# Linear attention of a transformer block: rolled tile loop and zero-padded value windows, or rounds over tiles with nine-column value matmuls

## The reference, cut to what matters

```python
x = x + _L0_attn_ref(_layernorm(x, axis=-1), L0_attn_Wqkv, L0_attn_bqkv, L0_attn_Wout, L0_attn_bout, L0_attn_proj)

def _L0_attn_ref(x, Wqkv, bqkv, Wout, bout, proj):     # H = 16 heads of D = 8, M = 64 features
    ...
    q_prime = jax.nn.relu(jnp.einsum('bhtd,hdm->bhtm', qf, pf))
    k_prime = jax.nn.relu(jnp.einsum('bhtd,hdm->bhtm', kf, pf))
    k_cumsum = jnp.cumsum(k_prime, axis=2)
    kv_prod = jnp.einsum('bhtm,bhtd->bhtmd', k_prime, vf)
    kv_cumsum = jnp.cumsum(kv_prod, axis=2)
    context = jnp.einsum('bhtm,bhtmd->bhtd', q_prime, kv_cumsum)
    norm = jnp.einsum('bhtm,bhtm->bht', q_prime, k_cumsum)
    out = context / (norm[..., None] + 1e-06)
    ...
    return out @ Wout.T + bout
```

## Time and profile before

| | us |
|---|---|
| median of 3 runs | 5663.83 |
| lowest and highest | 5661.9, 5679.79 |
| profiled execution, its own time | 5654.4 |
| its span in the trace | 5652.5 |
| the stage, from line 263 at 1096.98 to the end of line 2151 at 1733.37 | 636.4 |
| one round, 31 steps of line 2151 from 1138.1 to 1733.1 | 19.2 |

### The profile page before, as it was taken

One profiled execution on the slowest core, in us unless ns is written; L12 is line 12 of the kernel. 1 busy time (PEld: TensorE's weight loads), 2 busy tenths in 40 slices (PEclk: granted clock), 3 DMA queues, 4 the chain that ended last, 5 costly groups with the idle time before them and its releaser, 6 DMA issues.

```text
span 5652.5 us, 141251 instructions
## 1 busy us (share of the span) xinstructions
PE 4905.5 (87%) x49788; PEld 3894.9 (69%) x49788; DVE 3263.9 (58%) x9577; ACT 2087.9 (37%) x5175; POOL 1829.5 (32%) x2766
## 2 busy tenths in 40 slices
PE   5999999877878999999593999876999998986999
PEld 4777777677775777767462777665667777874776
DVE  4777777634344666656442666586456656765333
ACT  1444444311111444422130555442245554542333
POOL 2555555300000333323404334494023434430000
PEclk8999999999998999989695999897989998886999
DMA  5000000000000100000022111000310100004665
GB/s 189 18 18 18 19 18 18 10 0 0 0 0 12 31 29 29 25 1 0 23 69 54 31 33 34 16 0 2 89 35 30 34 27 0 0 0 78 143 145 134
DMA packets 112405, 199.22 MB, mean 35 GB/s; under 512 B 13315, under 2 KB 54660, under 8 KB 111260
## 3 DMA queue, kind: packets, MB, share of 16 engines
q1 hardware_dynamic: 108147, 188.67, 12.8%
q0 software_dynamic: 4096, 8.40, 0.5%
HBM read 183.29 MB, written 18.97 MB: 36 GB/s over the span
## 4 chain that ended last, share of the span: by engine, by line
PE 65%; issue 17%; DVE 7%; ACT 4%; POOL 3%; SPq 1%; DMA 1%; POOLq 1%; another core or an unknown queue 0%; DVEq 0%; ACTq 0%
PE psum_banks L2996 6%; PE psum_banks L555 6%; PE psum_banks L3005 6%; PE psum_banks L560 5%; PE psum_banks L620 4%; PE psum_banks L664 3%; PE psum_banks L671 3%; PE psum_banks L1623 3%; PE psum_banks L624 3%; PE psum_banks L1658 2%; PE psum_banks L1084 2%; PE psum_banks L2677 2%; PE psum_banks L1599 2%; ACT scratch L1741 1%; PE psum_banks L1072 1%
## 5 line engine op out<-in xcount | busy, mean ns | idle before, releaser
L787 DVE TENSOR_REDUCE scratch<-psum_banks 128x2 f32<-128x514 f32 x768 | 531.4, 692 | 406.9 <-PE psum_banks L555 402.9
L560 PE MATMUL psum_banks<-scratch 32*128 32x128 f32 x6144 | 637.6, 309 | 8.1 <-ACT scratch L706 6.1
L706 ACT ACTIVATE scratch<-psum_banks 128x512 f32<-128x512 f32 x768 | 458.7, 597 | 488.1 <-PE psum_banks L565 477.1
L555 PE MATMUL psum_banks<-scratch 32*128 32x257 f32 x3072 | 574.0, 440 | 50.8 <-DVE scratch L788 50.8
L560 PEld LDWEIGHTS psum_banks<-scratch 32*128 32x128 f32 x6144 | 475.0, 185 | 17.3 <-ACT scratch L706 8.6
L3005 PEld LDWEIGHTS psum_banks<-w_L_ffn_down,scratch 128*128 128x128 f32 (+1 forms) x2560 | 336.7, 193 | 165.1 <-issue 141.2
L555 PEld LDWEIGHTS psum_banks<-scratch 32*128 32x128 f32 x3072 | 253.9, 188 | 272.2 <-issue 172.7
L2996 PE MATMUL psum_banks<-scratch,w_L_ffn_up 128*128 128x512 f32 (+1 forms) x752 | 382.7, 604 | 8.3 <-DVE scratch L3167 6.0
L3052 ACT ACTIVATE scratch<-psum_banks 128x512 f32<-128x512 f32 x344 | 205.4, 597 | 485.0 <-PE psum_banks L2996 485.0
L3167 DVE TENSOR_TENSOR scratch<-scratch 128x512 f32<-128x512 f32 x304 | 210.3, 692 | 294.7 <-ACT scratch L3052 272.6
L565 PE MATMUL psum_banks<-shift_T,own_batch 32*128 32x128 bf16 x3072 | 350.5, 214 | 0.0
(11 more groups left out here) (475 smaller groups left out, 12748.6 us busy)
## 6 DMA issues: line engine op xcount, KB each, us to landing
scratch<-route_T SPq DMA_DIRECT2D x136, 512.0 KB, 7.1
scratch<-in_ctx SPq DMA_DIRECT2D x99, 514.0 KB, 3.5
scratch<-in_ctx_rows SPq DMA_DIRECT2D x130, 128.0 KB, 2.0
scratch<-route_T SPq DMA_DIRECT2D x8, 1024.0 KB, 8.3
expert_rows<-in_ctx SPq DMA_DIRECT2D x10, 512.0 KB, 17.5
scratch<-expert_rows SPq DMA_DIRECT2D x16, 192.0 KB, 2.7
expert_out<-scratch SPq DMA_DIRECT2D x16, 192.0 KB, 2.1
w_L_ffn_up<-in_L_ffn_up SPq DMA_DIRECT2D x1, 2992.0 KB
```

Of the source, the lines that this page charges most:

```text
L555: return pe.matmul(S[:, g % 2, :], qbd[q, t.odd, (s // 2) * P:(s // 2 + 1) * P], kT_of[q, t.odd, s // 2, :], start=True, stop=True)
L560: return pe.matmul(W[:, g % 2, c * P:(c + 1) * P], kT_of[q, t.odd, b, c * P:(c + 1) * P], qbd[q, t.odd, b * P:(b + 1) * P], start=True, st ...
L706: act.activation(pT[:, b % 2, 2 * h:2 * h + 2].rearrange("p t c q -> p t (c q)"), W, ACT.Exp).then_inc(exp_ready.sem, 1)
L787: dve.tensor_reduce(parts[:, r.t.odd, 2 * h:2 * h + 2, 0, b], S, X_AXIS, ALU.max, negate=True)
```

## The change

`linear_attention` is written anew; nothing else in the program changes.

- Values: each head's masked products `am` (128 x 128) are now the weights at rest, and nine columns stream past: the head's 8 value columns and a column of ones, from `v0` or `v1` (written by turns; the ones are set once). One group of 16 matmuls (`weigh`) gives numerators and denominators, tokens on the partitions, 16 x 9 columns in bank 6. `vz`, the window of ones, and the second group of 16 are gone.
- Since tokens are now on the partitions, the heads are transposed by TensorE (`turn_heads`) and copied by ScalarE (`take_heads`) ahead of the output matmul, which gives tokens on the partitions as before.
- VectorE divides with a 128 x 16 reciprocal instead of 128 x 128, and adds the output straight to `x`; the bias is added to `x` by GpSimd earlier (`biased`). ScalarE, not VectorE, takes the transposed norm out of PSUM (`take_x`).
- Products and masks go in halves: `multiply(t, 0)` and `multiply(t, 1)` fill one bank for the even and one for the odd heads each, and the mask is four instructions of 512 columns. `weigh` runs in four groups of four heads, each after its own mask, and the q features in two halves, each after the masks that have read its bank.
- The loop is unrolled into rounds -2 to 32: in round r TensorE works on x of tile r+2, features and v of tile r+1, products and values of tile r, transposed heads and output of tile r-1. All four uses of bank 7 have quarters of their own, yet `bank_free` still lets only one writing or reading of the bank be open at a time, in the order x, heads, v, out.

```diff
...
-def linear_attention(k, s):
...
+def linear_attention(k):
...
+    HEADS = O[:, 0:H * W].rearrange("p (h c) -> p h c", c=W)
+    values = (a["v0"], a["v1"])
+    X_AT, HEADS_AT, V_AT, OUT_AT = (slice(P * n, P * n + P) for n in range(4))
+
+    cols = lambda n: slice(n * P, (n + 1) * P)
+    there = lambda t: 0 <= t < TILES
+
+    def bank_of(odd, s):
+        return k.bank[(0 if odd else 4) + s]
+
+    events, order = {}, 0
+    for r in range(-2, TILES + 1):
+        for name, t in (("x", r + 2), ("heads", r - 1), ("v", r + 1), ("out", r - 1)):
+            if there(t):
+                order += 1
+                events[name, t] = order
...
+            if t:
+                pool.wait_ge(xn.sem, xn.at(t))
+                pool.tensor_tensor(k.X[:, t - 1, :], k.X[:, t - 1, :], bo[:, :], ALU.add).then_inc(biased.sem, 1)
...
-        with pe.Fori(0, TILES) as i:
-
-            pe.wait_ge(sg["q_features_ready"].sem, sg["q_features_ready"].at(i, 0))
-            pe.wait_ge(sg["k_features_ready"].sem, sg["k_features_ready"].at(i, 0))
-            for c in range(chunks):
-                for odd in range(2):
-                    rows = slice(64 * odd, 64 * odd + 64)
-                    mm = pe.matmul(product_bank(2 * c + odd), s["feature"][rows, 1, cols(c)], s["feature"][rows, 0, cols(c)],
-                                   start=True, stop=True, skip_group_check=True)
-                    if c == chunks - 1:
-                        mm.then_inc(sg["products_written"].sem, 1)
-            next_x(i)
-            features(1)
-            pe.wait_ge(sg["masked"].sem, sg["masked"].at(i, 2))
-            features(0)
-            pe.wait_ge(misc.r.sem, misc.r.at(i, 0))
-            for n in range(2):
-                for h in range(heads):
-                    if n == 0:
-                        left = s["vz"][:, 120 * h + 120:120 * h + 120 + P]
-                    else:
-                        left = k.c("head_window")[:, 120 - 8 * h:120 - 8 * h + P]
-                    mm = pe.matmul(O[:, cols(n)], left, s["am"][:, 8 * (h % 2) + h // 2, :],
-                                   start=(h == 0), stop=(h == heads - 1), skip_group_check=True)
-            mm.then_inc(sg["pv_done"].sem, 1)
-            next_v()
-            pe.wait_ge(sg["heads_ready"].sem, sg["heads_ready"].at(i, 1))
-            pe.wait_ge(misc.r.sem, misc.r.at(i, 2))
-            pe.matmul(M[:, 0:P], s["outT"][:, 0, :], wo[:, :], start=True, stop=True).then_inc(misc.w.sem, 1)
...
+        def bank_free(name, t):
+            if events[name, t] > 1:
+                pe.wait_ge(read.sem, read.at(events[name, t] - 1))
...
+        def turn_heads(t):
+            pe.wait_ge(heads_ready.sem, heads_ready.at(t + 1))
+            bank_free("heads", t)
+            pe.transpose(M[:, HEADS_AT], a["heads"], k.c("ident")).then_inc(written.sem, 1)
+
+        def project_v(t):
+            bank_free("v", t)
+            pe.wait_ge(read.sem, read.at(events["x", t]))
+            pe.matmul(M[:, V_AT], a["xT"][:, t % 2, :], wv[:, :], start=True, stop=True).then_inc(written.sem, 1)
+
+        def out(t):
+            bank_free("out", t)
+            pe.wait_ge(read.sem, read.at(events["heads", t]))
+            pe.matmul(M[:, OUT_AT], a["headsT"], wo[:, :], start=True, stop=True).then_inc(written.sem, 1)
...
+        def k_features(t):
+            pe.wait_ge(read.sem, read.at(events["x", t]))
+            if t:
+                pe.wait_ge(k_ready.sem, k_ready.at(t))
+            for c in range(F):
+                mm = pe.matmul(k.bank[2 + c // 4][:, cols(c % 4)], a["feature_w"][:, 1, cols(c)], a["xT"][:, t % 2, :],
                                start=True, stop=True, skip_group_check=True)
-            mm.then_inc(sg["q_features_written" if n == 0 else "k_features_written"].sem, 1)
-
-        pe.wait_ge(sg["proj_ready"].sem, sg["proj_ready"].before(1))
+            mm.then_inc(k_written.sem, 1)
+
+        def q_features(t, s):
+            if t:
+                pe.wait_ge(masked.sem, masked.at(4 * (t - 1) + 2 * s + 2))
+            for c in range(4 * s, 4 * s + 4):
+                mm = pe.matmul(k.bank[s][:, cols(c % 4)], a["feature_w"][:, 0, cols(c)], a["xT"][:, t % 2, :],
+                               start=True, stop=True, skip_group_check=True)
+            mm.then_inc(q_written.sem, 1)
+
+        def multiply(t, s):
+            if s == 0:
+                pe.wait_ge(k_ready.sem, k_ready.at(t + 1))
+            pe.wait_ge(q_ready.sem, q_ready.at(2 * t + s + 1))
+            for c in range(4 * s, 4 * s + 4):
+                for odd in range(2):
+                    rows = slice(64 * odd, 64 * odd + 64)
+                    mm = pe.matmul(bank_of(odd, s)[:, cols(c % 4)], a["feature"][rows, 1, cols(c)], a["feature"][rows, 0, cols(c)],
+                                   start=True, stop=True, skip_group_check=True)
+            mm.then_inc(products.sem, 1)
+
+        def weigh(t, n):
+            odd, s = parts[n]
+            pe.wait_ge(masked.sem, masked.at(4 * t + n + 1))
+            if n == 0:
+                pe.wait_ge(read.sem, read.at(events["v", t]))
+                if t:
+                    pe.wait_ge(heads_ready.sem, heads_ready.at(t))
+            for j in range(4):
+                h = 2 * (4 * s + j) + odd
+                mm = pe.matmul(HEADS[:, h, :], a["am"][:, 8 * odd + 4 * s + j, :], values[t % 2][:, h, :],
+                               start=True, stop=True, skip_group_check=True)
+            if n == 3:
+                mm.then_inc(heads_done.sem, 1)
...
+        for r in range(-2, TILES + 1):
+            if there(r):
+                multiply(r, 0)
+            if there(r + 2):
+                turn_x(r + 2)
+            if there(r):
+                multiply(r, 1)
+            if there(r + 1):
+                k_features(r + 1)
+            if there(r - 1):
+                turn_heads(r - 1)
+            if there(r):
+                weigh(r, 0)
+                weigh(r, 1)
+            if there(r + 1):
+                project_v(r + 1)
+                q_features(r + 1, 0)
+            if there(r):
+                weigh(r, 2)
+            if there(r - 1):
+                out(r - 1)
+            if there(r):
+                weigh(r, 3)
+            if there(r + 1):
+                q_features(r + 1, 1)
...
+        def take_heads(t):
+            act.wait_ge(written.sem, written.at(events["heads", t]))
+            act.activation(a["headsT"], M[:, HEADS_AT], ACT.Copy).then_inc(read.sem, 1)
...
+        for r in range(-2, TILES + 1):
+            if there(r + 2):
+                take_x(r + 2)
+            if there(r - 1):
+                take_heads(r - 1)
+            if there(r + 1):
+                q_features(r + 1, 0)
+                q_features(r + 1, 1)
...
-        with dve.Fori(0, TILES) as i:
-            chain.round(i)
-            norm.dve_stats(dve, chain, i)
-            norm.dve_apply(dve, i)
-            for odd in range(2):
-                dve.wait_ge(sg["products_written"].sem, sg["products_written"].at(i, odd + 1))
-                b = 4 if odd == 0 else 0
-                dve.tensor_tensor(s["am"][:, 8 * odd:8 * odd + 8, :].rearrange("p (a n) q -> p a n q", a=2),
-                                  k.psum[:, b:b + 2, :].rearrange("p a (n q) -> p a n q", q=P),
-                                  bc(bc(k.c("causal_T"), 1, 4), 1, 2), ALU.mult).then_inc(sg["masked"].sem, 1)
-                if odd == 0:
-                    prep_x(i)
-            k_features(i)
-            dve.wait_ge(sg["pv_done"].sem, sg["pv_done"].at(i, 1))
-            prep_v(i)
-            link(dve.tensor_scalar(s["den"][:, :], O[:, P:2 * P], 1e-6, None, ALU.add))
-            link(dve.reciprocal(s["den"][:, :], s["den"][:, :]))
-            dve.tensor_tensor(s["outT"][:, 0, :], O[:, 0:P], s["den"][:, :], ALU.mult).then_inc(sg["heads_ready"].sem, 1)
-            dve.wait_ge(misc.w.sem, misc.w.at(i, 3))
-            dve.tensor_tensor(s["tmp"][:, :], M[:, 0:P], bo[:, :], ALU.add).then_inc(misc.r.sem, 1)
-            dve.wait_ge(misc.r.sem, misc.r.at(i, 3))
-            x = k.X[:, i, :]
-            link(dve.tensor_tensor(x, x, s["tmp"][:, :], ALU.add))
...
+        def mask(t, n):
+            odd, s = parts[n]
+            if odd == 0:
+                dve.wait_ge(products.sem, products.at(2 * t + s + 1))
+            dve.tensor_tensor(a["am"][:, 8 * odd + 4 * s:8 * odd + 4 * s + 4, :], bank_of(odd, s).rearrange("p (n q) -> p n q", q=P),
+                              bc(k.c("causal_T"), 1, 4), ALU.mult).then_inc(masked.sem, 1)
...
+        def divide(t):
+            dve.wait_ge(heads_done.sem, heads_done.at(t + 1))
+            link(dve.tensor_scalar(a["den"], HEADS[:, :, 8], 1e-6, None, ALU.add))
+            link(dve.reciprocal(a["den"], a["den"]))
+            dve.tensor_tensor(a["heads"].rearrange("p (h d) -> p h d", h=H), HEADS[:, :, 0:8], bc(a["den"], 2, 8), ALU.mult
+                              ).then_inc(heads_ready.sem, 1)
+
```

(51 more changed lines are left out.)

131 lines of the change are left out of this document (67 added, 64 removed).

## The result

| | before | after |
|---|---|---|
| median of 4 runs, us | 5662.86 | 5401.63 |
| lowest and highest | 5656.76, 5679.79 | 5398.66, 5424.59 |
| span of the profiled execution | 5652.5 | 5396.9 |
| the stage in the trace | 636.4 | 384.4 |

The ratio is 0.9543, with a 95% interval of 0.951 to 0.9576. The forecast was 5405 within 5348 to 5461. Of the 255.6 us that the span lost, 252.0 are in the stage; the other 3.6 lie in parts that nobody touched.

A forecast was written before the change was run, and what follows sets the result against it. The prediction took TensorE's own work plus its waiting gaps to bound the stage. Set-up 22.2, 31 round steps x 11.2 = 347 and last tile 8.5 gave 378 us against 636.4, hence 5405 us, range 5348 to 5461.

The forecast's parts named there:

- set-up to the first products: Start of the stage until TensorE's first products: 22.2 us, against 23.4 before, as the head projection now leads.
- 31 round steps: Steady rounds of the unrolled loop: 10.5 us at full clock, 11.2 at clock 0.94, 347 us in all.
- last tile: End of the stage, no features behind it: products, masks, values about 5.5, then divide to residual 3; 8.5 us.
- The matmuls: TensorE per round: products 1.86, features, v and output 4.03, transposes 0.22, 32 nine-column instructions at 0.108, 3.46 us.
- rival A: Nine-column matmuls on TensorE are cheap, 0.058 instead of 0.108 us each: round 9.5, stage 325, total 5352 us; 8%.
- Hand-overs and the stall: TensorE per round: 13 semaphore waits at 0.055, 0.72 us, plus 0.2 waiting for ScalarE's late q features.
- The gaps: TensorE's old waits ahead of transpose 1.00, features 0.93 and output 1.97, together 3.9 us a round; nearly none remain.
- rival B: Bank 7 becomes the chain, TensorE waiting for its readers, a 1.97 us gap: round 13.3, stage 443, total 5470; 11%.
- The clock: TensorE's mean clock in the new rounds: 0.94, between two other stages' 0.85 and 1.00, making 10.5 us 11.2.
- my bound: Slow end of the main case: hand-overs 0.1 each and clock 0.85, round 13.0, stage 434, total 5461 us.
- C: Nine-column groups drop TensorE's clock to 0.50 for the whole stage: round 21 us, stage about 685, total 5712; 2%.
- D: Unrolled code arrives late or rounds do not overlap: round 17 us or more, total 5580 to 5680; 3%.

The follow-up runs named there:

- the last experiment: Against the changed kernel: 32 columns per head, both q feature groups moved right behind v, both product groups together with the norm's transpose behind them; 5338.93 us, ratio 0.9466.

## Why the prediction was right

The stage's first instruction, its first and its last tile's products, and its last instruction:

```profile
1095.70 1.23 DVE L2219 TENSOR_TENSOR scratch<-w_L_attn_proj,consts 128x1024 f32<-128x1024 f32 x1 [0.19 <-SPq L3356]
1121.94 1.16 PE L2091 MATMUL psum_banks<-scratch 64*128 64x128 f32 x16 [0.43 <-ACT scratch L2156]
1469.91 2.47 PE L2091 MATMUL psum_banks<-scratch 64*128 64x128 f32 x32
1479.84 0.29 DVE L2217 TENSOR_TENSOR x_tokens<-x_tokens,psum_banks 128x128 f32<-128x128 f32 x1 [1.86 <-PE psum_banks L2065]
```

Term by term, the sum against the profiled execution:

| | forecast | measured |
|---|---|---|
| set-up to the first products | 22.2 | 1121.94 - 1095.70 = 26.2 |
| 31 round steps | 347 | 1469.91 - 1121.94 = 348.0 |
| last tile | 8.5 | 1480.13 - 1469.91 = 10.2 |
| stage | 378 | 384.4 |

The mechanism held, but that forecast and median differ by only 3 us is partly luck. The stage was 6 us longer than forecast, 3.6 us fell away in parts that nobody touched, and the median lay 3.0 us above the profiled execution where I had added 9.4. Within a round two errors cancel as well: at full clock it is 10.34 us where I had 10.5, and its mean clock is 0.92 where I had 0.94.

- **The matmuls.** Nine-column matmuls at 0.108 were 0.107; rival A is out. With the value form exchanged alone, the round moved by 3.46 us, what the count says. The Trainium skill's 25 ns in "TensorE: Matmul & The Clock Gate", section "Back-to-back issue gap", are given without a weight load and are not what these matmuls take, which bring new weights each: 16 instructions take 1.71 us with nine columns and 1.70 with 32.
- **Hand-overs and the stall.** I spread 0.72 over 13 waits and added 0.2 for ScalarE, 0.92 together. Measured are 10.34 - 9.57 = 0.77, where 9.57 is the sum of the matmuls alone. The stall is there: the second products start at 1311.24, 0.10 after ScalarE's last activation ends (1310.00 + 1.14), where the transpose alone would have let them start at 1311.10, so 0.14. But the 13 waits are not alike. The value groups pay nothing (1318.05 - 1317.24 = 0.81 for 8), the product halves pay 0.17 each (1310.99 - 1309.89 = 1.10 against 0.93), and the q group ahead of the products another 0.16. The sum was nearly right and its place wrong: the cost sits at the products, and the last experiment took most of it away by moving two groups. That the cause is the change between 64- and 128-partition matmuls is my reading; the moved groups also changed the number of waits.
- **The gaps.** All three are gone, as the timeline shows, and no reader of bank 7 delays TensorE (rival B): VectorE had read v (L2204, until 1316.84) 1.2 us before the output needed its turn at 1318.05.
- **The clock.** I took 0.94 and a steady round of 11.2; measured 348.0 / 31 = 11.2. The reason behind it held: falls in spite of a busy TensorE, and only with the narrow streams. But 0.94 was an estimate between two other stages, so that it came this near is luck, and its shape was not foreseen: fewer falls than before (nine, against the 20 slow ones of 33 feature bursts that the prediction counts), with each costing 3.13 us instead of 1.63. In the second execution of the same kernel there were eleven, and its 31 steps took 354.2 us. A kernel in which every round had fallen would have been 70 us slower, above my bound. TensorE was busy 320 of 320 us at a clock of 0.92, and the same order with 32 columns got 1.00. The rule of the Trainium skill ("TensorE: Matmul & The Clock Gate", section "Why this matters for your kernels") that the clock holds as long as TensorE is not left idle between bursts does not agree with that.
- **The set-up** ran at a clock of 0.51 for nearly all of its length, where I had let it run as before; it took 4 us more than forecast. In the second execution of the same kernel it took 1117.78 - 1097.08 = 20.7 us, so the excess is not a fixed cost of the change. No experiment looked for the reason. The last tile was 1.7 us longer; its last groups ran at low clock too.
- **Rivals C and D** showed nothing: no stretch of the rounds stays at 0.50, and in the profile page's chain of work that ended last "issue" has 6% of the span where it had 17%. The larger of the two instruction queues fetched 127 packets instead of 102, and no round shows it.

What each part was worth, in us a round at full clock: from 18.08, the rounds over tiles 4.28, then the count of value matmuls 3.46. The clock took back 0.9 in the changed kernel (348.0 - 31 x 10.34 = 27.5 us), where the rounds with the old values lost nothing to it; the kernel before lost 19.2 - 18.1 = 1.1. Of the 4.28, 3.9 are the three gaps. They were closed by several edits at once (the norm further ahead, the divide a round later, halves, the bias on GpSimd, unrolling); only the halves were tried apart.

## What to carry to other kernels

Where every fp32 matmul brings its own 128 x 128 weights, a narrower stream saved next to nothing here (0.107 us an instruction with nine columns, 0.112 with 128), so make fewer of them, not narrower ones. Where the stream is short, try to pad it with columns that cost nothing: nine columns ran at a clock of 0.92, 16 and 32 at 1.00 and the same pace. Price a round by the start-to-start pace of each kind of matmul, then ask which of the others' results arrives last within it. A hand-over in halves hides what the other engine needs for its last half, here ScalarE's 1.14 us with its hand-over, 1.4 us of 10.3.

## What the runs showed that I had not expected

- Adding useless work made the kernel faster: 16 or 32 streaming columns instead of 9 gave 0.7% (ratios 0.9485 and 0.9487 against 0.955).
- With the narrow stream a low stretch lasts 6.8 us and costs 3.13; in the kernel before one slow burst cost 1.63. What makes it longer was not tried.
- In the old loop with nine columns the rounds settled at 17.07 us with a fall in each, so that halving the value matmuls alone gave 1.2% where I had expected 1.7 to 2.3%.
- The old loop with 32 columns has two outcomes: three executions at 5516 to 5517 us and one at 5571.63, with a lower clock.
